# Graph network megakernel: the edge features' product moves from the first aggregation layer into the edge network, and messages are summed as bf16 products of three parts

## The chip, the core and the metric

The kernel runs on one core of one Trainium2 chip. The metric is the device time of one execution, in microseconds (us), median of several runs. The engines of the core work beside each other, each in the order of its own instructions, and wait for one another by semaphores: TensorE (PE; PEld is its weight load), VectorE (DVE), ScalarE (ACT), GpSimd (POOL) and SyncE (SP), which here only issues DMAs.

## The reference, cut to what matters

Four graph layers run over 3125 nodes and 53125 edges sorted by destination, each followed by a residual and a layer norm. The first is a GIN with three rounds of plain neighbour sums. The second is the edge network, which the change is about; the third is an attention, the fourth a relational sum.

```python
# second layer
h = jnp.concatenate([x[row], edge_attr], axis=1)   # 64 node and 32 edge features
h = jax.nn.relu(h @ W1 + b1)                       # 96 -> 128
h = h @ W2 + b2
agg = scatter_mean(h, col, x.shape[0])
g = jnp.concatenate([x, agg], axis=1)
g = jax.nn.relu(g @ W3 + b3)
return g @ W4 + b4
```

The kernel uses that `h @ W1` is a product of `x[row]` (gathered from a table, 128 wide) plus a product of the edge features alone, and that `W2` can be applied after the mean.

## The kernel before, in words

**Blocks.** Nodes are cut into 25 blocks (`NT`) of 125. The edges that end in a block lie in 26 slots (`SB`) of up to 128 edges, a slot for each source block and one to spare. A gather or a sum over edges is a TensorE product with a 0/1 matrix of 128 edges by 125 nodes: `src_hot` picks source rows, `hot_in` sums messages by destination. fp32 values that must stay exact go through a bf16 product as three bf16 parts (`PIECES`): high, middle, low. `hi(x)` is the upper half of each fp32 word, read as bf16.

**Filing, 51 to 608 us.** POOL writes 416 tiles of edge records to `recs` in DRAM by indirect DMA (line 2174). The other engines crawl through their first blocks meanwhile.

**Layer one (`*_shadow`), up to about 906 us.** One step for each block `d`. SP loads the records (`recd`, line 2226), DVE makes the 0/1 matrices (line 2354), PE turns ids and features (lines 2369 and 2374) and forms the adjacency matrix in seven groups of up to four slots (line 2388), ACT copies the groups out (line 2531), SP stores them (line 2235) with the 0/1 matrix (line 2238) and ids (line 2241). PE multiplies adjacency by the node table (`pe_z`, line 2575). In the same step PE forms the edge features' product, 26 fp32 products of 32 rows (line 2459; `e1_half` 0 has 16, `e1_half` 1 has 10), ACT copies it to `e1_buf` (line 2479), and SP stores it as `e1_out` (line 2281). ACT packs the features of the next block (`act_pack`, line 2467) between the two halves, and for this waits for that block's records. SP's queue in a step is: load records of `d`, store adjacency, 0/1 matrix, ids and two halves of `e1` of `d-1`, then four small stores of segment rows of `d-2` (line 2264). The last block's product is formed at step 40, on its own (line 2489).

**Layers two and three of the GIN, 906 to 1056 us**, are products of stored adjacencies (`pe_z` again) with small tails.

**Edge network (`*_edge2`), 1080 to 1367 us.** 175 groups (`G7`), seven a block: six of four slots and one of two. In `step` PE gathers group `step` (line 2911, 12 bf16 products of 128 columns, three parts for each slot) into one of four PSUM banks; DVE adds the stored `e1` to it (line 3067), ACT applies relu (line 3014), and PE sums the group's messages three steps later (`LAG`; line 2923, fp32, 125 columns, messages stationary). POOL turns the 0/1 matrix into fp32 for that (line 2981). At the block's end DVE scales by one over the degree into `agg` (line 3083). Every four blocks the dense layers, layer norm and the attention's table follow, spread over fixed steps (`hid_step` and offsets).

## Time and profile before

| | us |
|---|---|
| median of 3 runs (1972.48 to 1977.16) | 1974.95 |
| the profiled execution | 1974.92 |
| its span, first to last instruction | 1973.6 |
| filing, other engines mostly idle | up to about 636 |
| layer one at full pace, block 2 on | 636 to 906 |
| GIN layers two and three | 906 to 1056 |
| edge network | 1080 to 1367 |
| attention, relational layer, end | 1367 to 1974 |

The profile's page divides the span by engine and by slice. Over the whole span PE is busy 65%, DVE 50%, ACT 31%, POOL 41% of the time; those shares mean little, as each stage has a limit of its own. The rows of the section below are read stage by stage. A matmul record is longer than the distance to the next one, since products are pipelined; the distance between starts is what a product costs.

### The profile page before, as it was taken

The numbers are of one execution on the slowest core, as the hardware profiler recorded it, in microseconds if no ns is written. First come the engines' busy times: TensorE is split into PE (matmuls) and PEld (weight loads), VectorE is DVE, ScalarE is ACT, GpSimd is POOL, SyncE is SP. The second block draws the span as 40 slices with busy tenths as digits, with TensorE's granted clock in tenths as the row PEclk, the third lists the DMA queues.
The fourth block names the chain that finished last, engine by engine and source line by source line (L and its number), as shares of the span: only waits on it lengthen the run. The fifth ranks groups of instructions, "written<-read, shape, count | busy, mean of one in ns | idle before, by whom it ended". The sixth has DMA issues, their size and how long they took to land.

```text
span 1973.6 us, 48209 instructions
## 1 busy us (share of the span) xinstructions
PE 1286.1 (65%) x20479; PEld 1175.4 (60%) x20480; DVE 979.0 (50%) x2196; ACT 618.1 (31%) x1433; POOL 806.2 (41%) x883
## 2 busy tenths in 40 slices
PE   6410000000002777778998999998799998989897
PEld 2300000000001666667897999998799998888896
DVE  7200020000001455554447555655788888888986
ACT  4000000000001777774213444343566666300000
POOL 1777777777772000000001444441010010388896
PEclk7555555555555999999997999998899999899999
DMA  7610000001102999997665788874666661344442
GB/s 230 241 35 15 15 15 14 13 14 48 34 14 75 349 357 359 352 346 272 239 253 198 279 302 310 312 293 176 255 242 238 224 244 52 141 165 158 170 177 89
DMA packets 89277, 360.69 MB, mean 183 GB/s; under 512 B 24940, under 2 KB 38431, under 8 KB 82079
## 3 DMA queue, kind: packets, MB, share of 16 engines
q1 hardware_dynamic: 75744, 349.84, 47.9%
q0 software_dynamic: 13312, 7.69, 1.7%
q8 instruction: 165, 2.70, 0.5%
q14 instruction: 56, 0.46, 0.1%
HBM read 250.77 MB, written 106.68 MB: 181 GB/s over the span
## 4 chain that ended last, share of the span: by engine, by line
PE 38%; another core or an unknown queue 22%; DVE 14%; issue 11%; ACT 7%; DMA 3%; POOL 2%; SPq 2%; ACTq 0%; DVEq 0%; POOLq 0%
PE ps L2923 8%; PE ps L2575 6%; PE ps L2911 6%; PE ps L3189 5%; PE ps L3542 4%; DMA arena<-recs 2%; DVE arena L2354 2%; PE ps L3556 2%; ACT arena L2479 2%; ACT arena L2531 2%; DVE arena L3607 2%; SPq L2264 2%; PE ps L2459 1%; POOL arena L3598 1%
## 5 line engine op out<-in xcount | busy, mean ns | idle before, releaser
L2174 POOL DMA_INDIRECT recs<-arena x416 | 425.6, 1023 | 173.2 <-issue 131.8
L2981 POOL CAST arena<-arena 128x512 f32<-128x512 bf16 (+1 forms) x175 | 119.2, 683 | 627.1 <-DMA arena<-hot_out 457.6
L2302 DVE TENSOR_TENSOR arena<-arena 128x25 f32<-128x25 int32 x25 | 4.9, 196 | 415.9 <-DMA arena<-recs 391.7
L3542 PE MATMUL ps<-arena 125*128 125x64 bf16 x5850 | 191.7, 194 | 8.8 <-issue 8.7
L2459 PE MATMUL ps<-wz,arena 32*128 32x128 f32 x1248 | 58.8, 319 | 208.9 <-ACT arena L2479 113.9
L3542 PEld LDWEIGHTS ps<-arena 125*128 125x128 bf16 x5850 | 186.5, 98 | 10.4 <-issue 9.9
L2923 PE MATMUL ps<-arena 128*128 128x125 f32 x1300 | 182.2, 282 | 0.0
L2459 PEld LDWEIGHTS ps<-wz,arena 32*128 32x128 f32 x1248 | 49.2, 215 | 221.1 <-ACT arena L2479 119.6
L3067 DVE TENSOR_TENSOR arena<-ps,arena 128x512 f32<-128x512 f32 (+1 forms) x175 | 114.3, 653 | 118.7 <-PE ps L2911 115.6
L3014 ACT ACTIVATE arena<-arena 128x512 f32<-128x512 f32 (+1 forms) x175 | 105.1, 601 | 171.8 <-DVE arena L3067 171.8
L2923 PEld LDWEIGHTS ps<-arena 128*128 128x128 f32 x1300 | 158.8, 192 | 0.0
L2479 ACT ACTIVATE arena<-ps 128x512 f32<-128x512 f32 (+1 forms) x192 | 83.6, 522 | 190.0 <-remote 142.5
L2911 PE MATMUL ps<-arena 125*128 125x128 bf16 x1950 | 139.5, 221 | 4.2 <-DVE arena L3054 4.2
L3595 POOL TENSOR_TENSOR arena<-arena 128x512 f32<-128x512 f32 x100 | 115.3, 1153 | 48.2 <-DVE arena L3675 48.1
L2911 PEld LDWEIGHTS ps<-arena 125*128 125x128 bf16 x1950 | 126.7, 99 | 9.1 <-issue 7.7
L2388 PE MATMUL ps<-arena 128*128 128x128 bf16 x625 | 56.7, 230 | 113.9 <-issue 51.2
L3189 PE MATMUL ps<-arena,y 128*68 128x125 f32 x984 | 121.9, 274 | 11.4 <-ACT y L3271 5.0
L2575 PE MATMUL ps<-agg,arena 125*128 125x193 bf16 (+1 forms) x1250 | 126.0, 255 | 1.1 <-DVE yn L2593 1.1
L2388 PEld LDWEIGHTS ps<-arena 128*128 128x128 bf16 x625 | 42.4, 103 | 128.3 <-issue 112.9
L3598 POOL TENSOR_TENSOR arena<-arena 128x512 f32<-128x512 f32 x100 | 112.8, 1128 | 7.8
L3189 PEld LDWEIGHTS ps<-arena,y 128*68 128x68 f32 x984 | 105.9, 141 | 15.1 <-issue 14.9
L3607 DVE TENSOR_SCALAR arena<-arena 128x3328 bf16<-128x3328 f16 x75 | 111.7, 1540 | 0.5 <-issue 0.3
(380 smaller groups left out, 2480.5 us busy)
## 6 DMA issues: line engine op xcount, KB each, us to landing
arena<-ids_out SPq DMA_DIRECT2D x100, 832.0 KB, 6.2
arena<-hot_out SPq DMA_DIRECT2D x75, 832.0 KB, 6.2
arena<-e_out SPq DMA_DIRECT2D x25, 1664.0 KB, 6.9
arena<-adj_out SPq DMA_DIRECT2D x41, 800.0 KB, 6.8
e_out<-arena SPq DMA_DIRECT2D x25, 1024.0 KB
hot_out<-arena SPq DMA_DIRECT2D x25, 832.0 KB, 7.6
adj_out<-arena SPq DMA_DIRECT2D x25, 800.0 KB, 5.8
e_out<-arena SPq DMA_DIRECT2D x25, 640.0 KB
```

The source lines that it names most:

```text
L2174: nc.gpsimd.indirect_dma_start(out=recs, out_offset=bass.IndirectOffsetOnAxis(ap=slot_row[:, t:t + 1], axis=0), in_=rec_in[:, t, :], in_of ...
L2459: ins = M(bank(r, HID, (g - 4 * half) * HID), attT[rows, g * 128:(g + 1) * 128], wz[rows, r * HID:(r + 1) * HID], start=True, stop=True, s ...
L2479: A(to[:, r:r + 4 * n - 3:4, :], bank(r, n * HID).rearrange("p (j h) -> p j h", h=HID), ACT.Copy)\
L2575: ins = M(to, blocks[0:NP_, k, :], yp[l % 2][:, k, 0:PIECES * C + (l == 0)], start=k == 0, stop=k == NT - 1, skip_group_check=True)
L2911: ins = M(bank(step % 4, HID, k * HID), src_hot[d % 2][0:NP_, j * SLOTS:(j + 1) * SLOTS], px[:, block_of(d, j), piece, :], start=piece == ...
L2923: ins = M(bank(4 + d % 2, NP_), act_out[s % 4][:, k * HID:(k + 1) * HID], hot_e[s % NH][:, k, 0:NP_], start=j == 0, stop=j == NT, skip_gro ...
L2981: nc.gpsimd.tensor_copy(hot_e[s % NH][:, 0:len(js), :], hot_in[d % 2][:, js[0]:js[0] + len(js), :])\
L3189: ins = M(bank(6 + d % 2, NP_)[0:ROW, :], xmsg[n % 3][:, k, :], hot32[(7 * d + j // 4) % NH][:, j % 4, 0:NP_], start=j == 0, stop=j == NT, ...
L3542: ins = M(bank(step % 4, C, k * C), hot_r[d % 2][r][0:NP_, j * SLOTS:(j + 1) * SLOTS], px3[:, block_of(d, j), piece, r * C:(r + 1) * C], s ...
L3595: nc.gpsimd.tensor_tensor(x[:, 1, 0:m], x[:, 0, 0:m], hi(x[:, 0, :])[:, 0:m], ALU.subtract)\
L3598: nc.gpsimd.tensor_tensor(x[:, 2, 0:m], x[:, 1, 0:m], hi(x[:, 1, :])[:, 0:m], ALU.subtract)\
L3607: V.tensor_scalar(hot_r[d % 2][r], row_r[d % 2], rel_at[:, r:r + 1], None, ALU.is_equal)\
```

## The change

**Layer one** no longer forms the edge features' product. SP stores the turned features themselves (`attr_out`, 128 by 896 fp32 values a block, 448 KB, in place of 1664 KB). On ACT `act_pack(d + 1)` now stands between the copies of adjacency groups 3 and 4 of block `d`. On PE groups 4 to 6 of the adjacency stand after the first 12 products of `pe_z`.

**Edge network, in.** PE works on four groups at a time (`pe_sums`), in four passes. A pass is up to four fp32 products of 32 rows, each with another quarter of the rows and in another bank, followed by the 12 gathered products that accumulate on them. DVE's addition and the loading of `e1` are gone. A batch waits until ACT has emptied all four banks.

**Edge network, out.** ACT applies relu straight from PSUM into one of five buffers of three parts; DVE forms the second and third part by two subtractions. The sum over edges is a bf16 product of 384 columns for each slot, with the stored 0/1 matrix stationary; POOL does nothing here any more. At the block's end DVE adds the three parts (a reduction) and scales, PE turns the result, ACT copies it to `agg`. `hid_step` is two steps later.

```diff
+                sp.wait_ge(sem("attr_turned"), d + 1)
+                sp.dma_start(attr_out[d], attT[d % 2]).then_inc(sem(f"attr_stored{d % 2}"), 16)
...
-                    if d < NT - 1:
-                        act_e1_half(act, d, 0)
-                        act_pack(act, d + 1)
-                        act_e1_half(act, d, 1)
+                        if g == 3 and d < NT - 1:
+                            act_pack(act, d + 1)
...
+        def turn_step(d):
+            return 7 * (d + 1) + LAG + 2
...
+        def pe_sums(pe, first):
+            d = min(first + 3, G7 - 1) // 7
+            pe.wait_ge(sem("src_hot"), d + 1)
+            pe.wait_ge(sem(f"attr_in{d % 2}"), 16 * (d // 2 + 1))
+            if first:
+                pe.wait_ge(sem("act_relued"), first)
+            cells, done = px_sums(first)
+            for i in range(4):
+                now = [(at, s, k) for at, (s, k) in enumerate(cells) if (s - first + i) % 4 == k]
...
+                    ins = M(bank(s % 4, HID, k * HID), attr_in[d % 2][rows, g * SLOTS:(g + 1) * SLOTS],
+                            wz[rows, k * HID:(k + 1) * HID], start=True, stop=False, skip_group_check=True)
...
+                        ins = M(bank(s % 4, HID, k * HID), src_hot[d % 2][0:NP_, j * SLOTS:(j + 1) * SLOTS],
+                                px[:, block_of(d, j), piece, :], start=False, stop=piece == 2, skip_group_check=True)
...
+                if step < G7 and step % 4 == 0:
+                    pe_sums(pe, step)
...
+                    pe.wait_ge(sem("act_low"), s + 1)
...
-                        ins = M(bank(4 + d % 2, NP_), act_out[s % 4][:, k * HID:(k + 1) * HID],
-                                hot_e[s % NH][:, k, 0:NP_], start=j == 0, stop=j == NT, skip_group_check=True)
+                        ins = M(bank(4 + d % 2, PIECES * HID)[0:NP_, :], hot_in[d % 2][:, j, 0:NP_],
+                                x[:, :, k * HID:(k + 1) * HID], start=j == 0, stop=j == NT, skip_group_check=True)
...
+                    if step == turn_step(d):
+                        pe.wait_ge(sem("agg_scaled"), d + 1)
...
-                    V.tensor_tensor(pre[step % 2][:, 0:m], bank(step % 4, m),
-                                    e1_in[d % 2][:, 4 * g * HID:4 * g * HID + m], ALU.add).then_inc(sem("e1_added"), 1)
+                    dve.wait_ge(sem("act_relued"), step + 1)
+                    V.tensor_tensor(x[:, 1, 0:m], x[:, 0, 0:m], hi(x[:, 0, :])[:, 0:m], ALU.subtract)\
+                        .then_inc(sem("act_left"), 1)
+                    dve.wait_ge(sem("act_left"), step + 1)
+                    V.tensor_tensor(x[:, 2, 0:m], x[:, 1, 0:m], hi(x[:, 1, :])[:, 0:m], ALU.subtract)\
+                        .then_inc(sem("act_low"), 1)
```

Three places show what moved. Line numbers are those of each kernel; in a row `to<-from` is what is written and read, then the size and the count.

ACT in one step of layer one, before: L2531 and L2530 are the adjacency copies, L2479 the copies of `e1`, L2467 is `act_pack` of the next block.

```order
L2531 ACTIVATE arena<-ps 128x512 x6
L2530 ACTIVATE arena<-ps 128x26
L2531 ACTIVATE arena<-ps 128x128
L2479 ACTIVATE arena<-ps 128x4x128 x4
L2467 ACTIVATE arena<-arena 128x832
L2479 ACTIVATE arena<-ps 128x3x128 x2
L2479 ACTIVATE arena<-ps 128x2x128 x2
```

The same step after: L2461 copies turned features, L2472 and L2471 are the adjacency copies, L2439 is `act_pack`.

```order
L2461 ACTIVATE arena<-ps 64x128
L2472 ACTIVATE arena<-ps 128x512 x4
L2439 ACTIVATE arena<-arena 128x832
L2472 ACTIVATE arena<-ps 128x512 x2
L2471 ACTIVATE arena<-ps 128x26
L2472 ACTIVATE arena<-ps 128x128
```

The packing of the next block has moved ahead of the last three adjacency copies, and the eight copies of `e1` are gone.

PE in the edge network, before: L2911 gathers a group, L2923 sums the one three steps back, L2934 and L2935 are dense layers.

```order
L2911 MATMUL ps<-arena 128x128 x12
L2923 MATMUL ps<-arena 128x125 x4
L2934 MATMUL ps<-xt_rows,w3_rows 128x500
L2935 MATMUL ps<-agg,w23 128x500
L2911 MATMUL ps<-arena 128x128 x6
L2923 MATMUL ps<-arena 128x125 x4
```

The same stage after: L2931 are the products of 32 rows, L2938 the gathered ones, L2859 the sums, L2867 is the turn of a block's means.

```order
L2931 MATMUL ps<-wz,arena 128x128 x3
L2938 MATMUL ps<-arena 128x128 x9
L2859 MATMUL ps<-arena 125x384 x12
L2867 MATMUL ps<-ident,arena 128x125
L2859 MATMUL ps<-arena 125x384 x4
L2931 MATMUL ps<-wz,arena 128x128 x4
L2938 MATMUL ps<-arena 128x128 x12
```

Gathers and sums no longer alternate group by group; four passes stand together, then four groups' sums, and the turn of the means stands among these.

DVE in the edge network, before: L3067 adds `e1`, L3054 makes `src_hot` of the next block, L3083 scales a block's sum.

```order
L3067 TENSOR_TENSOR arena<-ps,arena 128x256
L3067 TENSOR_TENSOR arena<-ps,arena 128x512 x2
L3054 TENSOR_SCALAR arena<-arena,pidx_f 128x3328
L3067 TENSOR_TENSOR arena<-ps,arena 128x512 x3
L3083 TENSOR_TENSOR agg<-ps,arena 128x125
```

The same place after: L3029 and L3032 are the two subtractions of a group, L3045 and L3050 are the reduction and the scaling on which PE's turn waits.

```order
L3029 TENSOR_TENSOR arena<-arena 128x512
L3032 TENSOR_TENSOR arena<-arena 128x512
L3045 TENSOR_REDUCE arena<-ps 125x128
L3050 TENSOR_SCALAR arena<-arena 125x128
L3029 TENSOR_TENSOR arena<-arena 128x512
L3032 TENSOR_TENSOR arena<-arena 128x512
L3029 TENSOR_TENSOR arena<-arena 128x256
L3032 TENSOR_TENSOR arena<-arena 128x256
```

Each group is two instructions instead of one, and the reduction for block `d` stands behind the subtractions of the fifth group of block `d+1`; PE's turn waits for it one step later. The table `src_hot` of the next block still stands behind the second group of a block (here four groups further on).

## Rows read from the trace of the kernel before

**Rows 1.** Busy time by stretch; columns as the first line names them.
```profile
core 0: us, PE busy (x) PEld busy (x) DVE busy (x) ACT busy (x) POOL busy (x), PEclk, DMA share, GB/s
636.00:906.00 270.00, 210.49 (x3174) 172.72 (x3172) 139.14 (x452) 204.70 (x494) 0.00 (x0) 0.93 0.94 352
906.00:1056.00 150.00, 147.94 (x1553) 132.71 (x1552) 72.98 (x192) 33.91 (x71) 0.00 (x0) 0.99 0.58 217
1080.00:1367.00 287.00, 286.85 (x3382) 279.21 (x3382) 166.99 (x289) 114.55 (x201) 113.76 (x167) 0.99 0.76 285
```

**Rows 2.** SP's DMA issues in layer one: start, duration, what was issued.
```profile
644.40 2.07 SPq L2264 DMA_DIRECT2D seg_out<-zeros  x4
646.64 0.35 SPq L2226 DMA_DIRECT2D arena<-recs  x1
...
853.02 0.99 SPq L2241 DMA_DIRECT2D ids_out<-arena  x1
...
858.46 4.37 SPq L2264 DMA_DIRECT2D seg_out<-zeros  x4
862.98 0.34 SPq L2226 DMA_DIRECT2D arena<-recs  x1
...
899.10 0.34 SPq L2226 DMA_DIRECT2D arena<-recs  x1
```

**Rows 3.** Timeline of DVE and ACT in layer one: start, duration, instruction, idle before.
```profile
650.19 0.20 DVE L2302 TENSOR_TENSOR arena<-arena 128x25 f32<-128x25 int32 x1 [6.10 <-DMA arena<-recs]
...
848.79 3.02 ACT L2531 ACTIVATE arena<-ps 128x512 bf16<-128x512 f32 x6
...
868.40 0.90 ACT L2467 ACTIVATE arena<-arena 128x832 f32<-128x832 f32 x1 [0.36 <-DMA arena<-recs]
```

**Rows 4.** ACT while records are filed.
```profile
592.56 1.43 ACT L2479 ACTIVATE arena<-ps 128x384 f32<-128x384 f32 x4 [53.16 <-remote]
```

**Rows 5.** PE in GIN layers two and three: start, duration, records.
```profile
942.79 2.23 PE L2575 MATMUL ps<-y,arena 125*128 125x192 bf16 x25
944.95 1.05 PE L2626 MATMUL ps<-arena,wgin 64*64 64x500 f32 x2
945.93 2.24 PE L2575 MATMUL ps<-y,arena 125*128 125x192 bf16 x25
...
958.99 6.22 PE L2489 MATMUL ps<-wz,arena 128*128 128x512 f32 x14
```

**Rows 6.** PE in the edge network, steady: gathers and sums.
```profile
1101.55 1.11 PE L2923 MATMUL ps<-arena 128*128 128x125 f32 x8
1102.50 0.83 PE L2911 MATMUL ps<-arena 125*128 125x128 bf16 x12
1103.17 1.11 PE L2923 MATMUL ps<-arena 128*128 128x125 f32 x8
```

**Rows 7.** PE in layer one: both halves of the edge features' product, and what follows.
```profile
840.66 1.17 PE L2459 MATMUL ps<-wz,arena 32*128 32x128 f32 x32 [0.35 <-ACT arena L2531]
841.76 1.19 PE L2575 MATMUL ps<-agg,arena 125*128 125x193 bf16 x12
...
844.07 0.94 PE L2459 MATMUL ps<-wz,arena 32*128 32x128 f32 x20 [1.12 <-ACT arena L2479]
844.94 0.76 PE L2575 MATMUL ps<-agg,arena 125*128 125x193 bf16 x7
```

**Rows 8.** PE in the relational layer: bf16 sums of 192 columns from three parts.
```profile
1764.54 0.88 PE L3556 MATMUL ps<-arena 128*125 128x192 bf16 x8
1765.26 2.26 PE L3542 MATMUL ps<-arena 125*128 125x64 bf16 x72
```

**Rows 9.** DVE in the attention: an fp32 operation on 512 values, and a table.
```profile
1506.37 0.69 DVE L3362 TENSOR_TENSOR y<-arena 128x512 f32<-128x512 f32 x1
1506.98 1.08 DVE L3132 TENSOR_SCALAR arena<-arena,pidx_f 128x3328 bf16<-128x3328 f16 x1
```

**Rows 10.** Groups of instructions, 1080 to 1367 us: busy, mean ns, idle before.
```profile
L3067 DVE TENSOR_TENSOR arena<-ps,arena 128x512 f32<-128x512 f32 (+1 forms) x175 | 114.3, 653 | 118.7 <-PE ps L2911 115.6 <-DVE yn L3094 1.0 <-DVE arena L3113 0.8
```

More of the change, by code:

```diff
@@ L276, in build @@
         px = e1_at([NP_, NT, PIECES, HID], BF16)
[L277 removed]
+        act_out = [e1_at([128, PIECES, 4 * HID]) for _ in range(4)]
         hot_in = [e1_at([128, SB, 128], BF16) for _ in range(2)]
[L279 removed]
         assert e1_at.at <= rest_at
@@ L283, in build @@
         e1_in0_at = e2_at.at
-        e1_in = [e2_at([128, SB * HID]) for _ in range(2)]
+        attr_in = [e2_at([128, 7 * SLOTS]) for _ in range(2)]
+        act_out += [e2_at([128, PIECES, 4 * HID])]
+        assert e2_at.at <= e1_in0_at + SB * HID
+        e2_at.at = e1_in0_at + 2 * SB * HID
         src_hot_at = e2_at.at
@@ L287, in build @@
         rcp_at = e2_at.at
-        rcp_row = [e2_at([128, CH * NP_]) for _ in range(2)]
+        agg_sum, agg_mean = e2_at([NP_, HID]), [e2_at([NP_, HID]) for _ in range(2)]
+        e2_at.at = rcp_at + 2 * CH * NP_
         p3_at = e2_at.at
@@ L291, in build @@
         assert e2_at.at >= sh.at
-        pre = [e2_at([128, 4 * HID]) for _ in range(2)]
+        e2_at.at += 2 * 4 * HID
         low_end, high_end = e1_at.at, e2_at.at
@@ L2816, in hid_step, with px_sums @@
         def hid_step(c):
-            return 7 * (tiles(c)[-1] + 1) + LAG + 2
+            return 7 * (tiles(c)[-1] + 1) + LAG + 4
+        def turn_step(d):
+            return 7 * (d + 1) + LAG + 2
+        def px_sums(first):
+            cells = [(s, (s - first + i) % 4) for i in range(4) for s in range(first, min(first + 4, G7))]
+            cells = [(s, k) for s, k in cells if k < len(groups(s // 7)[s % 7])]
+            last = {s: at for at, (s, k) in enumerate(cells)}
+            done, at = [0] * len(cells), 0
+            for s in sorted(last):
+                at = max(at, last[s])
+                done[at] += 1
+            return cells, done
         OUT, EVICT, ROOT, SCALED, TURN, TURNED, HUP, HIGH, LEFT, MID, LOW = 3, 4, 9, 11, 13, 15, 17, 19, 21, 23, 25
@@ L2902, in pe_edge2 @@
             for step in range(E_STEPS):
-                if step < G7:
-                    d, g = divmod(step, 7)
-                    if g == 0:
-                        pe.wait_ge(sem("src_hot"), d + 1)
-                    if step >= 4:
-                        pe.wait_ge(sem("e1_added"), step - 3)
-                    for k, j in enumerate(groups(d)[g]):
-                        for piece in range(PIECES):
-                            ins = M(bank(step % 4, HID, k * HID), src_hot[d % 2][0:NP_, j * SLOTS:(j + 1) * SLOTS],
-                                    px[:, block_of(d, j), piece, :], start=piece == 0, stop=piece == 2,
-                                    skip_group_check=True)
-                    ins.then_inc(sem("px_got"), 1)
+                if step < G7 and step % 4 == 0:
+                    pe_sums(pe, step)
                 if LAG <= step < G7 + LAG:
@@ L3010, in act_edge2 @@
                     m = HID * len(groups(d)[g])
-                    act.wait_ge(sem("e1_added"), step + 1)
-                    if step >= 4:
-                        act.wait_ge(sem("act_summed"), step - 3)
-                    A(act_out[step % 4][:, 0:m], pre[step % 2][:, 0:m], ACT.Relu).then_inc(sem("act_relued"), 1)
+                    act.wait_ge(sem("px_got"), step + 1)
+                    if step >= 5:
+                        act.wait_ge(sem("act_summed"), step - 4)
+                    A(act_out[step % 5][:, 0, 0:m], bank(step % 4, m), ACT.Relu)\
+                        .then_inc(sem("act_relued"), 1)
+                for d in range(NT):
+                    if step == turn_step(d):
+                        act.wait_ge(sem("agg_turned"), d + 1)
+                        A(agg[:, d * NP_:(d + 1) * NP_], bank(4 + d % 2, NP_, PIECES * HID), ACT.Copy)\
+                            .then_inc(sem("agg_read"), 1)
                 for c in range(NCH):
```

209 lines of the change are left out of this document (73 added, 136 removed).

## The prediction

> **What bounds the kernel now.** I read the busy time by stretch first [rows 1], then the queue or engine that is full in each stretch.
>
> In the edge network PE is busy 286.85 of 287 us at a clock of 0.99 of full speed, DVE 166.99, ACT 114.55: PE is the bound and the others wait for it, DVE 115.6 us for the gathers [rows 10]. A group of four costs 1.62 us: eight fp32 records of the sum 0.95 (1101.55 to 1102.50), 12 gathered products 0.67 (1102.50 to 1103.17) [rows 6]. So a slot is 0.056 x 3 = 0.17 us of gather and 0.2375 us of sum, a block of 26 slots 4.35 + 6.17 = 10.5 us, 25 blocks 263 us; the other 24 us are dense layers.
>
> In layer one at full pace no engine is full (PE 210, ACT 205, DVE 139 of 270 us), but the DMA engines are busy 0.94 [rows 1]. The step is 22 loads of records from 646.64 to 899.10, so 252.5 / 21 = 12.02 us [rows 2]. What repeats is a loop through SP: records land, ACT packs them, the rest of the block's work is copied out and stored, four segment stores are issued, and only then SP issues the next load. In the two GIN layers PE is full again (147.94 of 150 us) [rows 1].
>
> **Layer one.** Eight copies on ACT, 26 products on PE and 1664 KB of stores a block go; 448 KB of stores come. None of that was the limit alone; the loop was. The new loop, for one block: landing of the records 3.55 us in the first step (646.64 to 650.19) and 5.42 later (862.98 to 868.40) [rows 2, 3], I take 4.0, near the quiet one, since the bytes of a step fall by 30%. Packing 0.90 [rows 3], 0.85 to the next start. Three adjacency copies, now behind the packing: six take 3.02 us [rows 3], so 1.45 for the last three with the degree column. Then four stores: ids took 0.99 [rows 2], the others 0.3 to 0.6, together 2.25. Four segment stores: 2.07 us in the quiet step, 4.37 in a full one [rows 2], I take 2.8. With 0.15 for the load it is 11.5 us, 0.5 less than 12.02; over 23 steps **-12 us**. The ends: with the quiet values 10.3 us (-39), with 5.0 and 3.3 us for landing and segments 12.9 (+20). What is late next is still SP's queue. By the DMA volume alone a step could be far shorter, so this is where I could be too pessimistic.
>
> The Trainium skill ("DMA: Bandwidth & Descriptors", Latency and other measured facts) says that the fixed cost of a DMA shrinks with lighter load on the memory. The two landings above agree in direction; by that rule one would take 3.55 us, and the total would be 10 us lower.
>
> **Start.** While records are filed every engine crawls; the second half of block 0's `e1` was copied at 592.56 after 53.16 us idle [rows 4]. Without those copies and products block 1 should be through by then instead of at 636: I take one step, **-12 us**, between 0 and -24.
>
> **The last block's product** (line 2489) stood in the full PE stretch, 958.99 to the next start 6.06 us later, 14 records of 0.43 [rows 5]. It goes: **-6 us**.
>
> **Edge network, PE's work.** Per block 26 sums become bf16 products of 384 columns. Rows for it: 192 columns cost 0.082 us in the GIN (25 from 942.79 take 2.06) [rows 5], and 0.090 where the operand is the upper halves of fp32 words (8 from 1764.54 to 1765.26) [rows 8]; twice that is 0.165 to 0.18, I take 0.172. Saved: 650 x (0.2375 - 0.172) = **-43 us**.
>
> The edge features' product comes in: 44 batches of four passes, 176 passes. In layer one 16 products (four passes) took 1.10 us to the next product's start and 10 (three passes) 0.87 [rows 7], so 0.23 a pass and some 0.18 once. That 0.18 is the way back to products that use all rows. The same shows around line 2626, two products of 64 rows: the 25 before it end at 942.79 + 2.06 = 944.85, it starts at 944.95; its own streaming is 2 x 0.417 = 0.83 (500 columns, against 0.43 for 512 in the row of line 2489), and the next starts at 945.93, so 0.10 going in and 0.15 coming out [rows 5]. In layer one that was paid twice a block; here each pass is alone between full-height products. A pass is 0.10 + 0.23 + 0.16 = 0.49 us, and 176 are **+86 us**; with no switching cost they would be 40, with every pass at 0.31 (in, or out, hidden) 55.
>
> The Trainium skill ("TensorEngine Tiling (Array Packing)", Key Properties) says "Mode switching requires drain": going from one way of dividing the array's rows to another empties it. This speaks against the change, as 352 switches are added; the gaps of line 2626 agree. A reading of the same page by the speed of packed products alone would give the 40 us.
>
> 25 turns of the means, one product each at 0.1 to 0.24 us: **+4**. PE's work: -43 + 86 + 4 = +47 us.
>
> **Edge network, waits.** Before, PE waited for nobody. Now four groups end together. Call T the end of a batch of passes. ACT empties a bank in 0.5 us after the other, the first by T + 0.35 (its last product comes half a microsecond earlier). DVE needs two dependent fp32 operations of 512 values a group: 0.69 with its end waited for, then 0.61 to the next start (1506.37 to 1506.98) [rows 9]: 1.32 a group, the first ready at T + 1.85, the next ones at 3.2, 4.5, 5.8. Meanwhile PE has four groups' sums of 0.69 each, three of them older ones, so the fresh one is wanted at T + 2.06: no wait of itself.
>
> The turn is another matter. PE turns a block's means at step 7(d+1) + 5 and waits for DVE's reduction, which stands behind the subtractions of step 7(d+1) + 4. If the turn falls on a batch's first step, all is ready. On the second PE is there at T + 1.4, DVE has done group 0 and then 0.9 us of reduction and scaling, T + 2.75; on the third 4.05 against 2.06; on the fourth 5.4 against 2.75. Waits of 0, 1.4, 2.0 and 2.6, equally often since 7 and 4 share no factor: 1.5 a block, less what later waits would have cost anyway, **+35 us**.
>
> `src_hot` (1.08 us on DVE [rows 9]) stands behind the second group of a block; in one block of four the next batch wants it when DVE gets to it at T + 4.2 and PE is ready at 2.75. With smaller cases **+10 us**. DVE's own load is 25 x (6 x 1.32 + 0.79) for the subtractions, 218 us, plus the 166.99 - 114.3 of other work [rows 1, 10] and 15 for reductions: 285 us of the stretch, 11.4 a block. It has hardly slack, so it comes late to some batches: **+10 us**. The last batch's subtractions and turn have nothing beside them: +3. POOL's conversions are gone but were hidden behind PE; ACT has fewer us than before.
>
> Edge network: 47 + 35 + 10 + 10 + 3 = **+105 us**, so some 392.
>
> **Sum.** 1973.6 - 12 - 12 - 6 + 105 = 2048.6 us span, 1.3 us outside it (1974.92 against 1973.6), **2050 us**; the profiled run stands at the median of before (1974.95).
>
> **Rivals.**
> A. DMA relief decides layer one. For it: the DMA engines are 0.94 busy and lose 1.2 MB of 4.0 a step; against it: the loop above contains the packing and twelve issues that no bandwidth shortens. With the quiet values everywhere -39 instead of -12, and two steps at the start: 2050 - 27 - 12 = 2011 us.
> B. PE hides the switching and DVE keeps ahead (the other side). If the weights of the next product load across a switch, a pass is 0.23 us and the work is -43 + 40 + 4 = +1; if the turn's wait falls into slack, waits are near 0. Then 2050 - 104 = 1946 us. It decides below an edge network of 317 us, where the gains elsewhere (30 us) pay for it. Against it: the measured gaps, and a reduction that stands behind fresh subtractions by program order.
> C. Half of B: passes at 0.31 and half of the waits, -31 - 27: 1992 us.
> D. DVE or SP are worse: subtractions at 0.72 both, the loop at 12.9 us, PE at half clock after some waits (it is 0.93 in layer one, where it waits often [rows 1]): 2050 + 15 + 32 = 2097 us.
> E. The four products of a pass don't overlap, so each costs like an fp32 product of the old sum, 0.2375 us: 154 us instead of 86, 2118 us. The 1.10 us for 16 speak against it.
>
> **How the numbers follow.** Chances: forecast 0.6 (2020 to 2080 by its own bounds), A 0.13, B 0.07, C 0.1, D 0.07, E 0.03. The range 1988 to 2085 leaves out B, most of D, and E. A measurement here tells about 0.2%, 4 us, from no change: faster 0.09 (B and the lower end of C), same 0.03, slower 0.88.
>
> **What would show it.** Of the after profile: the edge network 370 to 410 us long; distance from the first product of 32 rows to the first gathered one some 0.33 us and a gap of about 0.1 before it; PE waiting for DVE's scaling some 35 us; PE busy about 85% there. Layer one's records loaded every 11 to 12 us, with DMA share near 0.7. No line like 2489 in the GIN layers. I am wrong if the passes' pitch is near 0.23 us, if PE's waits stay under 20 us, or if the step of layer one is under 10.3 us.

## The result: 2103.2 us, 6.5% slower, and the profile after

| | us |
|---|---|
| median after (2102.62 to 2103.77) | 2103.18 |
| median before, with one run more (1972.48 to 1977.16) | 1973.90 |
| ratio, 95% interval | 1.0647 (1.0634 to 1.066) |
| span of the profiled execution | 2102.0 (before 1973.6) |

The direction was forecast, the size was not: 2050 us with a range to 2085. The trace says where the 128.4 us of span are. The first product of the edge network starts at 1075.6 (before 1079.9), the attention's first gather at 1506.1 (before 1376.7), and from there to the end it is 595.9 us (before 596.9). So the stages ahead of the edge network gave back 4 us, and the edge network cost 134.

Busy time by stretch, the answer to [rows 1]; columns as there.

```profile
core 0: us, PE busy (x) PEld busy (x) DVE busy (x) ACT busy (x) POOL busy (x), PEclk, DMA share, GB/s
636.00:903.00 267.00, 181.09 (x1866) 152.98 (x1865) 135.13 (x438) 123.37 (x296) 0.00 (x0) 0.74 0.67 245
903.00:1055.00 152.00, 147.38 (x1610) 135.24 (x1609) 78.55 (x207) 33.77 (x72) 0.00 (x0) 0.99 0.57 216
1075.60:1506.00 430.40, 380.82 (x4078) 290.13 (x4078) 289.39 (x512) 108.65 (x235) 0.00 (x0) 0.91 0.36 125
```

In the edge network PE is no longer full: 380.8 of 430.4 us, at a clock of 0.91. The same stretch before, up to the attention, has 291.84 of 297.1 us at 0.98. PE's busy time rose by 89 us and its idle time by 44. (That stretch is taken to 1377; from the first product to the attention's first gather it is 296.8 us.)

PE at full clock, the place of [rows 6]: a batch of four passes (L2931, L2938) and the sums (L2859).

```profile
1099.06 0.50 PE L2931 MATMUL ps<-wz,arena 32*128 32x128 f32 x8
1099.50 0.84 PE L2938 MATMUL ps<-arena 125*128 125x128 bf16 x12
1100.27 0.50 PE L2931 MATMUL ps<-wz,arena 32*128 32x128 f32 x8
```

First product of a pass to the first gathered one 0.44 us; gathers to the next pass 0.77, where 12 of them alone take 0.67: so 0.10 going in, and a pass costs 0.54.

PE a little later, at a turn of the means (L2867) and behind it.

```profile
1117.46 2.69 PE L2859 MATMUL ps<-arena 128*125 128x384 bf16 x14
1122.70 0.47 PE L2867 MATMUL ps<-ident,arena 125*128 125x125 f32 x1 [2.55 <-DVE arena L3050]
1123.10 0.81 PE L2931 MATMUL ps<-wz,arena 32*128 32x128 f32 x8
1123.85 1.46 PE L2938 MATMUL ps<-arena 125*128 125x128 bf16 x12
1125.24 0.81 PE L2931 MATMUL ps<-wz,arena 32*128 32x128 f32 x8
1125.98 1.46 PE L2938 MATMUL ps<-arena 125*128 125x128 bf16 x12
```

After a wait of 2.55 us for DVE's scaling the same pass takes 0.75 instead of 0.44 us and the same gathers 1.39 instead of 0.77: PE runs at half its clock (1.2 in place of 2.4 GHz) for the next products. This is the term that my sum did not have. Not every wait is followed by it. Behind a wait of 1.37 us a little later the same pass takes 0.43 us, as at full clock:

```profile
1154.02 0.50 PE L2931 MATMUL ps<-wz,arena 32*128 32x128 f32 x6 [1.37 <-DVE arena L3019]
1154.45 0.68 PE L2938 MATMUL ps<-arena 125*128 125x128 bf16 x9
```

Nor does it slow behind 1.83 us at 1218.26 (0.43). Behind 2.56 us at 1189.92 the first pass takes 0.44 us and the second 0.75.

DVE beside it: two subtractions a group, then the reduction and the scaling.

```profile
1121.17 0.69 DVE L3032 TENSOR_TENSOR arena<-arena 128x512 f32<-128x512 f32 x1
1121.78 0.55 DVE L3045 TENSOR_REDUCE arena<-ps 125x128 f32<-125x384 f32 x1
1122.36 0.28 DVE L3050 TENSOR_SCALAR arena<-arena 125x128 f32<-125x128 f32 x1
1122.57 0.68 DVE L3029 TENSOR_TENSOR arena<-arena 128x512 f32<-128x512 f32 x1
```

What PE waited for from 1075.6 to 1506 us: us, times, longest.

```profile
PE ps L2867 <- DVE arena L3050: 28.9, 19, 2.6
PE ps L2931 <- DVE arena L3019: 13.8, 7, 4.3
PE ps L2931 <- ACT arena L2973: 3.1, 6, 0.7
PE ps L2859 <- DVE arena L3032: 2.9, 6, 1.7
```

In layer one the 22 loads of records run from 641.53 to 902.55 us: 12.43 us a step, where [rows 2] had 12.02. SP's queue for a step of it, the answer to [rows 2]: four stores, four segment stores, load (L2228), then 5 us of waiting.

```profile
789.97 0.34 SPq L2228 DMA_DIRECT2D arena<-recs  x1
790.36 0.43 SPq L2269 DMA_DIRECT2D arena<-adj_out  x1
795.55 0.32 SPq L2237 DMA_DIRECT2D adj_out<-arena  x1
795.92 0.43 SPq L2240 DMA_DIRECT2D hot_out<-arena  x1
796.39 0.93 SPq L2243 DMA_DIRECT2D ids_out<-arena  x1
797.36 1.20 SPq L2246 DMA_DIRECT2D attr_out<-arena  x1
798.61 3.95 SPq L2265 DMA_DIRECT2D seg_out<-zeros  x4
802.72 0.34 SPq L2228 DMA_DIRECT2D arena<-recs  x1
```

What ACT waited for at the packing, in the kernel before (646 to 900 us):

```profile
ACT arena L2467 <- DMA arena<-recs: 3.7, 6, 0.9
```

and in the changed one (641 to 903 us):

```profile
ACT arena L2439 <- DMA arena<-recs: 119.7, 21, 7.0
```

Before, ACT waited for records in 6 of the steps, 3.7 us in all. Now it waits in every step, 119.7 us. For ACT the landing was covered by the copies of `e1`; it is now in the open. DVE waited for the same records in both kernels, and long; in the kernel before:

```profile
DVE arena L2302 <- DMA arena<-recs: 90.1, 17, 8.0
```

What those waits of DVE were worth is seen in e14.

### The profile page after: what moved, and what is told of

Read it like the earlier page. It is cut to its first block, busy times and chain, and to the rows that moved or that the text cites. A ratio compares the mean times of both kernels' runs of the same rounds, so it can differ in the third digit from the quotient of the medians.

```text
span 2102.0 us, 46555 instructions
## 1 busy us (share of the span) xinstructions
PE 1362.7 (65%) x19892; PEld 1170.2 (56%) x19893; DVE 1097.0 (52%) x2398; ACT 526.0 (25%) x1259; POOL 687.2 (33%) x708
## 4 chain that ended last, share of the span: by engine, by line
PE 33%; issue 22%; DVE 22%; another core or an unknown queue 10%; ACT 4%; DMA 3%; SPq 3%; POOL 2%; ACTq 0%; DVEq 0%; POOLq 0%
PE ps L2512 6%; PE ps L2938 6%; PE ps L3508 4%; PE ps L3156 4%; PE ps L2931 4%; DVE arena L2349 4%; DMA arena<-recs 3%; SPq L2265 3%; DVE arena L3029 2%; PE ps L2859 2%; PE ps L3522 2%; DVE arena L3573 2%; DVE arena L3032 1%; DVE arena L3099 1%
## 5 line engine op out<-in xcount | busy, mean ns | idle before, releaser
L3311 POOL TENSOR_TENSOR y<-y 128x104 f32<-128x104 f32 x25 | 9.3, 372 | 1108.8 <-ACT y L3289 1108.8
L2425 PE MATMUL ps<-arena 128*128 128x128 bf16 x625 | 79.2, 289 | 210.0 <-issue 167.1
L2425 PEld LDWEIGHTS ps<-arena 128*128 128x128 bf16 x625 | 59.7, 132 | 232.0 <-issue 176.5
L3029 DVE TENSOR_TENSOR arena<-arena 128x512 f32<-128x512 f32 (+1 forms) x175 | 113.6, 649 | 129.6 <-ACT arena L2973 129.1
L2512 PE MATMUL ps<-agg,arena 125*128 125x193 bf16 (+1 forms) x1250 | 142.1, 275 | 53.2 <-issue 44.9
L2938 PE MATMUL ps<-arena 125*128 125x128 bf16 x1950 | 156.9, 236 | 0.0
L2512 PEld LDWEIGHTS ps<-agg,arena 125*128 125x128 bf16 x1250 | 119.5, 109 | 64.8 <-issue 50.7
L2938 PEld LDWEIGHTS ps<-arena 125*128 125x128 bf16 x1950 | 124.0, 106 | 24.3 <-issue 6.5
L2472 ACT ACTIVATE arena<-ps 128x512 bf16<-128x512 f32 (+1 forms) x175 | 88.0, 549 | 184.3 <-remote 87.0
L2859 PE MATMUL ps<-arena 128*125 128x384 bf16 x650 | 128.1, 337 | 3.1 <-DVE arena L3032 2.9
L3032 DVE TENSOR_TENSOR arena<-arena 128x512 f32<-128x512 f32 (+1 forms) x175 | 114.4, 654 | 6.0
L2931 PE MATMUL ps<-wz,arena 32*128 32x128 f32 x1300 | 97.5, 350 | 17.1 <-DVE arena L3019 13.8
```

Source lines behind the costliest of these rows:

```text
L2425: ins = M(to, hot_s[d % 2][:, j, :], hot_d[d % 2][:, j, :], start=True, stop=j != d, skip_group_check=True)
L2512: ins = M(to, blocks[0:NP_, k, :], yp[l % 2][:, k, 0:PIECES * C + (l == 0)], start=k == 0, stop=k == NT - 1, skip_group_check=True)
L2859: ins = M(bank(4 + d % 2, PIECES * HID)[0:NP_, :], hot_in[d % 2][:, j, 0:NP_], x[:, :, k * HID:(k + 1) * HID], start=j == 0, stop=j == NT, ...
L2931: ins = M(bank(s % 4, HID, k * HID), attr_in[d % 2][rows, g * SLOTS:(g + 1) * SLOTS], wz[rows, k * HID:(k + 1) * HID], start=True, stop=Fa ...
L2938: ins = M(bank(s % 4, HID, k * HID), src_hot[d % 2][0:NP_, j * SLOTS:(j + 1) * SLOTS], px[:, block_of(d, j), piece, :], start=False, stop= ...
L3029: V.tensor_tensor(x[:, 1, 0:m], x[:, 0, 0:m], hi(x[:, 0, :])[:, 0:m], ALU.subtract)\
```

## The experiments

Some groups of runs ran where the filing proceeds beside layer one and the whole program is about 300 us shorter (the kernel before took 1668 and 1674 us there, not 1974 to 1977). The edge network takes the same on both: 296.8 us in the kernel before, and 296.7 in e11, which is that kernel with a change in layer one alone and ran in a group of the shorter kind. Each ratio below is to the kernel before in the same group, and across groups I compare the length of the edge network: first product of a batch to the attention's first gather.

| kernel | edge network | PE busy | clock | PE idle | ratio to before, 95% |
|---|---|---|---|---|---|
| before | 297.1 | 291.8 | 0.98 | 5.3 | 1 |
| changed | 430.4 | 380.8 | 0.91 | 49.6 | 1.0647 (1.0634 to 1.066) |
| changed, again (e5) | 422.8 | 372.3 | 0.93 | 50.5 | 1.0644 (1.0619 to 1.0669) |
| turn later (e1) | 380.5 | 355.0 | 0.97 | 25.5 | 1.0498 (1.0449 to 1.0547) |
| table early (e2) | 407.2 | 363.9 | 0.95 | 43.3 | 1.0661 (1.0642 to 1.068) |
| both (e3) | 369.4 | 350.8 | 0.98 | 18.6 | 1.0415 (1.0392 to 1.0437) |
| passes together (e4) | 453.3 | 390.4 | 0.88 | 62.9 | 1.0941 (1.0922 to 1.0961) |
| bank by rows (e6) | 413.0 | 343.9 | 0.89 | 69.1 | 1.0554 (1.0537 to 1.0572) |
| no features (e7) | 350.3 | 281.5 | 0.91 | 68.8 | 1.0259 (1.0233 to 1.0284) |
| e3 and e6 (e9) | 333.0 | 313.3 | 0.97 | 19.7 | 1.0133 (1.0116 to 1.015) |

**The changed kernel again (e5).**

> The changed kernel itself, beside the edits below, because the first four runs ran with another filing stage (the kernel before took 1668.3 us there, not 1974). Edge network (first 32-row product to the attention's first gather) 430 us as in the first trace; difference to the kernel before between 125 and 133 us on either kind of run.

Median 2101.28 us, 124.2 over the kernel before (1977.13), just under what I had written, and the edge network 422.8 us. Idle time is the same as in the first trace, the clock is 0.93 against 0.91: two executions of one kernel differ by 8 us in PE's busy time. So a length set against the changed kernel has two values below, by its first trace and by e5.

**Waits: the turn later, the table early, both (e1, e2, e3).** From one group, e1 and e2 each with one of these edits.

```diff
-            return 7 * (tiles(c)[-1] + 1) + LAG + 4
+            return 7 * (tiles(c)[-1] + 1) + LAG + 6
...
-            return 7 * (d + 1) + LAG + 2
+            return 7 * (d + 1) + LAG + 4
```

```diff
                     x = act_out[step % 5]
+                    if g == 0 and d + 1 < NT:
+                        src_tables(d + 1)
...
-                if step < G7 and d + 1 < NT:
-                    if g == 1:
-                        src_tables(d + 1)
```

> Edit to the changed kernel: PE's turn of a block's means and ACT's copy of it stand two steps later (and the dense layers with them). Theory W (waits and the clock): PE waits 28.9 us at the turn, 19 times, and about 34 us more are lost because products run at half clock after waits. With two steps more DVE's reduction is done before PE comes: the wait at the turn falls under 5 us, the clock of the stretch rises from 0.92 to about 0.96, 29 + 17 us come back and two steps at the end cost 3: about 2060 us. Rival S (DVE has no slack): what PE no longer waits for at the turn it waits for at the sums (third part) and at the table; waits stay near 48 us and the time within 8 us of 2103.

> Edit to the changed kernel: DVE makes the next block's src_hot before the subtractions of a block's first group, where it idles, and not behind the second group. Theory W: the waits of the 32-row passes for the table (13.8 us, 7 times) go, and their share of the clock loss with them (about 9 us): about 2080 us, turn still 29 us of waits. Rival S: the table merely delays the subtractions that follow, the waits move to the turn: within 8 us of 2103.

> Both edits: turn two steps later, table before the first group. Theory W: hardly a wait longer than 0.5 us is left in the edge network, the granted clock there is at least 0.98, and all of 49 us of waits and 34 us of clock come back but 3 us at the end and some 5 us of first and last batch: about 2028 us (from 2103). If waits go but the clock stays at 0.92 the clock has another cause: about 2060. Rival S: 2090 or more.

Medians 1746.73, 1777.20 and 1737.89 us beside 1668.28 (the changed kernel itself was not timed there, so their ratios are not to be held against its 1.065, only against each other's and e4's). The times named in the expectations were for the 1974 us kind; the lengths can be compared. In e1 no wait of the turn is left and the edge network is 50 us shorter than in the first trace (42 by e5); in e2 it is 23 (16) shorter; in e3 61 (53). What PE waited for in e3, from 770.6 to 1140 us:

```profile
PE ps L2931 <- ACT arena L2973: 6.7, 13, 0.6
PE ps L2931 <- DVE arena L3019: 6.1, 6, 4.3
PE ps L2859 <- DVE arena L3034: 2.7, 2, 1.7
```

The rival that DVE has no slack falls: the waits did not move to the subtractions (2.7 us against 2.9). Theory W holds in kind: 31 us of idle time went, and PE's busy time fell by 30 (22 by e5) although PE had the same instructions to do, as the clock rose from 0.91 (0.93) to 0.98. Busy time times clock is nearly the same in all five, 344 to 347 us, so it is the clock that differs and not the work. The clock followed the waits, and cost two thirds of what they did or as much again. Its size was less than I wrote, 61 or 53 of the expected 75, as some 19 us of waits remain where the kernel before had 5.

**The passes together (e4).** The 16 products of 32 rows of a batch stand ahead of all gathered ones; each pass still waits for the one before.

```diff
                 ins.then_inc(sem("e1_begun"), 1)
-                for at, s, k in now:
+            pe.wait_ge(sem("e1_begun"), first + 4)
+            for i in range(4):
+                now = [(at, s, k) for at, (s, k) in enumerate(cells) if (s - first + i) % 4 == k]
+                for at, s, k in now:
```

> Edit to the changed kernel: the four passes of 32-row products of a batch stand together ahead of all 48 gathered products, so PE goes from whole-height to 32-row products and back once a batch and not four times. Each pass still waits for the products of the one before. Theory D (each change between the two heights costs 0.10 us going in and some 0.2 coming out): a batch's passes cost 0.10 + 4 x 0.23 + 0.2 = 1.2 us in place of 4 x 0.54 = 2.16, 44 batches give back 40 us: about 2063 us. Rival P (a pass itself, or waiting for its end, takes the 0.44 us): 4 x 0.44 + 0.10 = 1.86, 13 us back: about 2090 us.

This kernel drops part of the edge features' product: all four column blocks of a bank are started before any has its gathered rows, so that only the one started last keeps it. The Trainium skill ("PSUM — Partial Sum Buffer", The four PSUM rules) says that a product that starts a sum clears the written marks of its whole bank, so that the open sums beside it are overwritten. No trace shows the marks; the number and kind of instructions are those of the changed kernel, so the time can be read.

It was worse than both theories, 453.3 us. A batch in it:

```profile
904.75 2.27 PE L2931 MATMUL ps<-wz,arena 32*128 32x128 f32 x32 [0.47 <-ACT arena L2976]
907.11 2.85 PE L2941 MATMUL ps<-arena 125*128 125x128 bf16 x48
```

Four passes take 2.36 us, 0.59 each. In the changed kernel the wait for the pass before has 12 gathered products in between and costs nothing; here each pass stands still until the last one is written. So neither theory was tested yet: the wait had to go.

**A quarter of rows tied to a bank (e6).** The slot decides the bank and the step the columns, so the 16 products need no wait among them; only the first of a bank carries the start flag. ACT reads a group out of four banks.

```diff
-                    ins = M(bank(s % 4, HID, k * HID), attr_in[d % 2][rows, g * SLOTS:(g + 1) * SLOTS],
-                            wz[rows, k * HID:(k + 1) * HID], start=True, stop=False, skip_group_check=True)
+                    M(bank(k, HID, s % 4 * HID), attr_in[d % 2][rows, g * SLOTS:(g + 1) * SLOTS],
+                      wz[rows, k * HID:(k + 1) * HID], start=k not in seen, stop=False, skip_group_check=True)
+                    seen.add(k)
...
-                    A(act_out[step % 5][:, 0, 0:m], bank(step % 4, m), ACT.Relu)\
+                    A(act_out[step % 5][:, 0, 0:m].rearrange("p (k h) -> p k h", h=HID),
+                      bank(0, 4 * BANK).rearrange("p (k n) -> p k n", n=BANK)
+                      [:, 0:m // HID, step % 4 * HID:(step % 4 + 1) * HID], ACT.Relu)\
```

> Edit to the changed kernel: a quarter of rows always writes the same PSUM bank (bank k, column block of the step), so the 16 products of 32 rows of a batch follow each other with no wait between them, then the 48 gathered ones; only the first product of a bank carries the start flag. Theory D (of a pass's 0.54 us 0.23 is streaming, the rest changing heights): a batch costs 0.10 + 4 x 0.23 + 0.2 = 1.2 us in place of 2.16, 43 us shorter an edge network: about 387 us. Theory P (each pass takes 0.44 us whatever stands around it): 1.86 a batch, 417 us. From the run with the passes together but waiting, where four took 2.27 us, I hold D for right and the waiting for the cause of its loss.

Median 2084.70 us beside 2101.28 for e5 in the same group. A batch of 14 slots in it:

```profile
1189.10 1.16 PE L2929 MATMUL ps<-wz,arena 32*128 32x128 f32 x28
1190.20 2.52 PE L2936 MATMUL ps<-arena 125*128 125x128 bf16 x42
1192.55 0.85 PE L2859 MATMUL ps<-arena 128*125 128x384 bf16 x4
```

The 14 products take 1.10 us to the first gathered one, and 42 gathers 2.35, their bare 0.056 each. A batch of 16 slots takes 1.11 us to its first gathered one (1155.40 to 1156.51). With 0.10 going in that is 1.2 us where four passes cost 2.16: theory D was right on PE's work, and PE is busy 28 us less although at a lower clock. But the edge network is only 10 us shorter, and not 43, as PE's idle time rose from 50.5 to 69.1; the rest of the 17 us of the whole kernel lies outside it. What it waited for, from 1076 to 1489 us:

```profile
PE ps L2867 <- DVE arena L3049: 37.5, 25, 2.6
PE ps L2929 <- DVE arena L3018: 14.3, 7, 4.3
PE ps L2859 <- DVE arena L3031: 13.3, 14, 2.2
```

What PE saves it waits for DVE, half of it at the turn (37.5 us for 29.7 in e5) and half at the sums, for the third part (13.3 for 2.9), and it pays with the clock, 0.89 for 0.93.

**Without the features' products (e7).** The 32-row products are left out, so the messages lack the edge features' part.

> The changed kernel without the products of 32 rows (the edge features' part is left out of the messages; the gathered products start the sums; everything else stays, loads too). It prices all that the passes cost: 176 x 0.54 = 95 us of PE. If PE's time is what sets the edge network, it is 430 - 95 = 335 us. If DVE's order sets it, PE only waits longer in turn: waits for the reduction and the table rise from 49 us by 20 to 40, the granted clock falls below 0.92, and the edge network stays at 355 to 380 us.

The passes' whole price is seen in PE's busy time, 91 us less than in e5 (95 expected). The edge network fell by 73 to 350.3, a little under the lower edge of what I gave for the case in which DVE's order matters: idle time rose by 18 us, where I had 20 to 40. Even with no switching and no feature product at all the changed order is 53 us longer than the kernel before.

**Three edits (e9).** e3 and e6 together.

> The changed kernel with three edits of the edge network together: turn two steps later, table before the first group, a quarter of rows tied to a bank. Alone they left the edge network at 381 us (turn), 407 (table), 369 (both) and 413 (rows and banks, where PE's work fell by some 42 us and its waits rose by 19), from 423 to 430. Theory W: with the waits gone PE's shorter work counts in full: 369 - 42 + 5 = 332 us, 90 to 98 less than the changed kernel, about 2007 us where that takes 2101; still above the 296.8 of the kernel before, whose PE never waits. Rival S (DVE's work and order are the next limit): 350 us or more, with PE waiting over 25 us for the subtractions (lines of the third part).

333.0 us, within 1 us of theory W. PE has 21.5 us more to do than in the kernel before and waits 14 more. Median 1698.09 us, 1.3% above the 1674.24 of the kernel before in its group.

**Layer one: the load a step earlier (e8).**

```diff
-            for step in range(NT + 1):
-                if step < NT:
-                    d = step
+            for step in range(-1, NT + 1):
+                if step + 1 < NT:
+                    d = step + 1
```

> Edit to the changed kernel: SP issues the load of a block's records one step earlier, ahead of the stores and the four segment stores it used to follow. Theory L (layer one's step is a loop through landing 3.4, packing 0.8, last copies 1.4, stores 3.1, segment stores 3.3, load 0.2 = 12.2 us): landing and segment stores leave the loop and the step falls to some 8 us where filing is over, bounded by SP's own 7 us of issues and DVE's 6: about 90 us less in a run in which layer one follows the filing (1974 us kind), and little where layer one runs beside the filing (1668 us kind), since there POOL sets its step. Rival B (DMA bandwidth sets the step, as its share of 0.67 could hide): landing grows as fast as it is taken out, under 20 us in either kind.

Median 2037.09 us, ratio 1.0301 (1.0281 to 1.0321), 64 less than e5. The loads run from 642.07 to 826.90 us in 20 steps, 9.2 us each. Theory L holds, short of its 8 us; another wait came up, and the DMA share of the stretch is 0.89. What DVE waited for there, from 642 to 827 us:

```profile
DVE iota_i L2309 <- DMA hot_out<-arena: 49.6, 18, 6.7
```

The 0/1 matrix cannot be made before the store of the one two blocks back has landed.

**The same in the kernel before (e11, e14).** The first ran where the filing lies beside layer one and says nothing on this.

> The kernel before with only the earlier load of records. Its step of 12.0 us held the landing (5.4 in full pace), packing, the rest of the copies and the same stores; the DMA engines were 0.94 busy. If the loop set the step, as in the changed kernel, some 50 us come back: about 1925 us. If the DMA engines set it, under 15 us: 1962 or more. I hold the second for likelier here: 4.0 MB a step at 352 GB/s are 11.4 us, so the step can't fall by more than 0.6 us, 14 in all.

There it took 1687.15 us, 1.008 (1.006 to 1.01) of the kernel before.

> The kernel before with the records loaded one step earlier, once more, for a run in which layer one follows the filing. Theory B (the DMA engines set its step: 4.0 MB at 352 GB/s are 11.4 us against a step of 12.0): under 15 us, 1962 or more, ratio 0.993 to 1.0. Theory L (the loop set it): some 50 us, ratio 0.975. In a run of the other kind 1.008 again.

1971.66 us, ratio 0.9983 (0.9971 to 0.9994): the time is theory B's, and the loop through SP did not set the step. That the DMA engines did is not shown by it. Their share in e14 from 642 to 890 us is 0.95:

```profile
642.00:890.00 248.00, 195.96 (x2962) 161.23 (x2954) 139.28 (x439) 190.69 (x463) 0.00 (x0) 0.93 0.95 359
```

But ACT waited for a DMA only twice there, and for PE all the time:

```profile
ACT arena L2481 <- PE ps L2461: 41.5, 41, 2.4
ACT arena L2481 <- DMA e_out<-arena: 4.7, 2, 2.8
PE ps L2461 <- ACT arena L2481: 20.0, 21, 1.6
```

ACT's 190.7 us of work and its 57 of waits fill the 248 us, and PE in turn waited for ACT's copies of `e1`, and 16.3 us for those of the adjacency. In the chain that ended last from 646 to 890 us these copies and PE's products have most of the time, and the landing of a store of `e1` 8%. DVE's waits for records are gone, and the step is 11.77 us for 12.02: with the loop through SP taken away, PE and ACT waiting for each other hold it nearly where it was. I had overlooked this, and how much the DMA engines add to it no run separates. Both parties of that exchange lost work by the change: 26 products and eight copies a block.

**The features' store first (e12, e15).** It stands ahead of the other three stores of the step.

> The changed kernel with the store of the turned features ahead of the other three stores of the step and not behind them. It takes SP 1.2 us where I had reckoned some 0.6. Theory F: its 1.2 us is its own (448 KB of fp32 with the turned features' 3.6 KB rows) and it leaves the loop, since the features are ready long before the last adjacency copy: step 12.4 - 1.2 = 11.2 us, 26 us less, about 2075. Theory Q: the time is that of the fourth store in a row, whatever it is (a full queue): then the ids' store, now last, takes 1.2 us or more and the segment stores as long as before: the step falls by at most 0.5 us, 2090 or more.

1808.73 us, 1.0787 (1.0763 to 1.0811), in a group of the other kind: inconclusive, since the records' loads there are 17 us or more apart whatever SP does (17.0 in e1 too), and the changed kernel itself was not timed in such a group.

> The changed kernel with the turned features stored ahead of the other three stores, once more, for a run in which layer one follows the filing. Theory F (the 1.2 us are its own, and leave the loop): step 12.3 to 11.1 us, 26 us less, ratio to the kernel before 1.051. Theory Q (a full queue; the time moves to the stores behind it): under 8 us, ratio 1.060 or more.

2083.74 us, ratio 1.0543 (1.0515 to 1.0571), 17 us less than e5, between the two theories but nearer F. SP in it:

```profile
799.97 0.34 SPq L2228 DMA_DIRECT2D arena<-recs  x1
800.36 0.44 SPq L2269 DMA_DIRECT2D arena<-adj_out  x1
800.84 1.36 SPq L2237 DMA_DIRECT2D attr_out<-arena  x1
806.14 0.32 SPq L2239 DMA_DIRECT2D adj_out<-arena  x1
806.50 0.43 SPq L2242 DMA_DIRECT2D hot_out<-arena  x1
806.98 0.93 SPq L2245 DMA_DIRECT2D ids_out<-arena  x1
807.95 3.29 SPq L2265 DMA_DIRECT2D seg_out<-zeros  x4
```

The store has left the loop and the ones behind it take what they took: the step is 11.6 us (638.07 to 881.31 in 21), 0.8 less. Its own duration ranges from 0.32 to 1.42 us, median 0.43, against a median of 1.21 as the fourth: the same store is as a rule dearer behind three others (the one in these rows took 1.36).

**All four edits (e10, e13).** e9 and e8.

> The same with the load of records one step earlier in layer one too (that edit alone gave 64 us). The stages don't overlap, so the gains add: about 1943 us where the changed kernel takes 2101 and the kernel before 1977; that would be 1.7% below the kernel before. If the edge network is held by DVE, 1965.

It ran where the filing lies beside layer one: 1710.65 us, 1.0225 (1.0198 to 1.0252); the early load made it 13 us longer there than e9.

> The four edits together once more (turn later, table early, rows tied to banks, records loaded a step earlier), for a run in which layer one follows the filing (the kernel before takes 1974 us). The edge network took 333 us with the first three where the changed kernel takes 423 to 430, and the load alone gave 64 us: 2101 - 64 - 94 = 1943 us, a ratio of 0.983 to the kernel before. In a run of the other kind (1670 us) I expect 1.022 again, since the early load costs 14 us there.

1933.15 us (1930.19 to 1936.89) beside 1976.34: ratio 0.9783 (0.9763 to 0.9803). Where layer one follows the filing this beats both kernels, by 2.2 and by 8%. Its edge network is 330.5 us, still 34 more than before, and begins 73 us earlier (1006.5 for 1079.9). That gain is in layer one and needs both parts: the early load alone gave the kernel before 5 us, and the change alone made the step longer. The step is 9.2 us at a DMA share of 0.89. The bytes of the kernel before, some 4.2 MB a step by its 352 GB/s, would be 460 GB/s in 9.2 us (an estimate), and no stretch shown here has more than 359.

## Why the prediction was wrong

The time is 53 us above the forecast: some 29 of it in the edge network, and 26 because the stages ahead gave back 4 us where I had 30 (the end is 1 us shorter).

**Edge network: 134 us for 105.** By the same parts:

- *PE's work, +47 forecast, +59 measured* (350.8 us in e3 at the clock of 0.98 that the kernel before had with 291.8). The pass was mis-sized by little: 0.54 for my 0.49, since coming out takes 0.2 and not 0.16, 176 x 0.05 = 9 us; the other 3 I can't place. The idea of the term, that a change of height costs more than the products, is borne out by e6: 1.2 us for what cost 2.16. It isn't the change between fp32 and bf16, since 12 gathers between fp32 sums in [rows 6] take 0.056 us each, as the 42 in a row of e6 do. e6 also drops the waits between passes; passes kept apart without them were not run. The rule of "TensorEngine Tiling (Array Packing)" that the prediction quoted from the Trainium skill pointed the right way, its speed alone (40 us for all passes) would have missed 55.
- *Waits, +58 forecast, +44 measured.* The turn 28.9 (35), the table 13.8 (10), the third part 2.9 (10). Of the table's, 4.3 is the first one of the stage, which the kernel before has too (4.2), so the new ones are 9.6. e1 and e2 show that the turn's and the table's waits hang on the order of the instructions. I had DVE with hardly any slack: it is busy 289 of 430 us, and with the same 289 the edge network of e3 is 61 us (53 by e5) shorter, by another order alone.
- *The clock, 0 forecast, some 30 measured* (380.8 - 350.8, e3 against the changed kernel; 22 by e5). This step failed. I had it in rival D alone, with a chance of 0.07, though [rows 1] had PE at 0.93 where it waits. Each wait was priced at its length; the rows behind 1122.70 show that the next products can cost nearly double. That the waits are the cause is shown by e3, and in the longer kind of run by e13, which has a clock of 0.99 with 32-row products in it.

Rival D's time (2097) was nearest, 6 us off, in part by luck. Its half clock and its longer loop are there, but the loop's 32 us were 20 (+8.5 for -12), and the 15 left for slower subtractions and the clock are less than the clock alone, 22 to 30. Rival E's 2118 has a reason that is not there: the four products of a pass do overlap, 14 in 1.10 us.

**Layer one: +8.5 us forecast as -12.** The new loop has the members that I listed, and e8 shows it, but three sizes were wrong: landing 3.4 to 3.5 (4.0 taken), four stores 3.1 (2.25 taken, the features' store 1.2 and the ids' 0.93 in it), segments 3.3 (2.8 taken), in all 12.3 for 11.5. The step that failed more deeply is "what repeats is a loop through SP" for the kernel before: ACT waited 3.7 us for records there, and e14 gained 4.7 us where the loop would have given 50. What e14 shows in its place is PE and ACT waiting for each other, at a DMA share of 0.95. The change shortened that exchange and took bytes off the DMA engines (0.94 to 0.67), but the packing had been moved to where the landing is in the open, and the loop, now the longer path, took what they gave. On the Trainium skill's rule ("DMA: Bandwidth & Descriptors", Latency and other measured facts) that latency shrinks with load the trace agrees: 3.4 us (789.97 to 793.41), as in the quiet step.

**Start: -5 for -12.** Block 1's last adjacency copy is at 634.72 us, and was at 636.59: the engines crawl until filing is over, whatever is taken from them. The first load in full pace is 5 us earlier. **The last block's product: -6** is within the 7.7 us by which the way from the last load to the edge network is shorter (173.1 for 180.8).

Of the signs that I named, the edge network (430 for 370 to 410) and the pass (0.44 for 0.33) were off, the wait for the scaling (28.9 for 35), PE's share (0.88 for 0.85) and DMA share (0.67) came out; the loads' pitch, 12.4, lies outside 11 to 12.

## What to carry to other kernels

Price a wait of PE at its length and at the half-speed products that can stand behind it; over the edge network the second came to two thirds of the first or as much, and shortening PE's work by some 40 us without removing the waits made the stage only 10 shorter. Products of 32 rows between whole-height ones pay for the change both ways, so gather them into one block, with each quarter of rows on its own bank, or the waits between them eat the gain. Before a step is called a loop, take one member out and time it. The waits alone mislead: of the two engines that use the records DVE waited 90 us for them and ACT 3.7, and in e14 DVE's waits went for a gain of 5 us. A change that moves a consumer can put it into the loop, as it did ACT. A DMA share of 0.94 is no proof either that the DMA engines set the step.

## What the runs showed of the hardware

- A pass of four 32-row fp32 products between whole-height ones costs 0.54 us, of which about 0.23 is streaming (an estimate from the 1.10 and 0.87 us of [rows 7]). Waiting for the pass before, with nothing between, costs 0.59 a pass; without waits 14 products take 1.10 us.
- After a wait of 2.55 us the next products ran at the lower of PE's two clocks, 1.39 for 0.77 us; after waits of 1.37 and 1.83 us elsewhere they did not (0.43 us a pass). Two executions of one kernel with equal waits had 0.91 and 0.93 of the clock there.
- The same 448 KB store took SP 1.21 us (median) as the fourth in a row and 0.43 as the first.
- With the DMA engines at 0.94 to 0.95, loading earlier gave 0.2%; with them at 0.67 the same edit gave 64 us and raised their share to 0.89. In the first case PE and ACT waited for each other in every step (ACT 41.5 us for the products of `e1`, PE 20.0 for their copies).
- Where filing by POOL ran beside layer one, the same kernel was 300 us faster, and the edit that gained 64 us cost 13. What decides which kind a run is, no run here shows.
